# A four-layer Flamingo block: dense experts turned into experts by routing, with the routing inside the second attention and an unrolled feed-forward

## The reference, cut to what matters

```python
x = x + tanh(g_xattn[0]) * attention0(ln(x), ctx, ctx)       # 16 heads of 8
x = x + tanh(g_ffn[0])   * feed_forward0(ln(x))              # quantised rows, 128 -> 512, depthwise conv, silu, 512 -> 128
x = x + tanh(g_xattn[1]) * attention1(ctx, ln(x))            # latents attend to context and latents, 16 heads of 64, layer norm
x = x + tanh(g_ffn[1])   * experts(ln(x))

def experts(x):                                              # E = 8 experts, K = 2 chosen per row, 256 hidden
    gate = x @ Wg.T
    top_v, top_i = top_k(gate, 2)
    probs = softmax(top_v)
    for e in range(8):
        w_e = sum(probs * (top_i == e))                      # zero for the six that were not chosen
        h1, h2 = x @ W1[e].T, x @ W2[e].T
        out += (h1 * sigmoid(h1) * h2) @ W3[e].T * w_e
```

## Time and profile before

| | us |
|---|---|
| median of three runs | 1413.82 |
| lowest, highest | 1412.66, 1414.06 |
| the profiled execution, its own time | 1411.43 |
| its span, first to last instruction | 1409.6 |
| PE busy (granted clock 0.894 of full on average) | 1197.1 |
| DVE busy | 1099.3 |
| ACT busy | 930.5 |
| POOL busy | 856.1 |

### The profile page before, as it was taken

One profiled execution on the slowest core, in us unless ns is written; L12 is line 12 of the kernel. 1 busy time (PEld: TensorE's weight loads), 2 busy tenths in 40 slices (PEclk: granted clock), 3 DMA queues, 4 the chain that ended last, 5 costly groups with the idle time before them and its releaser, 6 DMA issues. The chain is left out here.

```text
span 1409.6 us, 39591 instructions
## 1 busy us (share of the span) xinstructions
PE 1197.1 (85%) x14741; PEld 902.5 (64%) x14741; DVE 1099.3 (78%) x2878; ACT 930.5 (66%) x1858; POOL 856.1 (61%) x823
## 2 busy tenths in 40 slices
PE   1578999949984599999999999999994688888887
PEld 1445777735652488888887878787873355555555
DVE  5888888867988666777767686868674799998996
ACT  0668999836654488778787878787872455454554
POOL 0251999942207366676666666666663477777778
PEclk9879555559995799999999999999997799999999
DMA  9100000000000021111111112111111000000000
GB/s 229 54 1 1 13 16 17 16 9 1 1 1 0 1 32 32 32 29 32 28 32 32 31 26 32 32 32 28 32 29 23 0 1 9 8 7 7 7 8 16
DMA packets 104027, 33.09 MB, mean 23 GB/s; under 512 B 88468, under 2 KB 102204, under 8 KB 103868
## 3 DMA queue, kind: packets, MB, share of 16 engines
q1 hardware_dynamic: 92827, 27.50, 9.6%
q10 hardware_dynamic: 11040, 3.42, 1.0%
HBM read 9.92 MB, written 2.10 MB: 9 GB/s over the span
## 5 line engine op out<-in xcount | busy, mean ns | idle before, releaser
L1173 POOL TENSOR_TENSOR attention_pl_l<-attention_probs_l,attention_ph_l 128x512 f16<-128x512 f32 x128 | 148.0, 1157 | 180.6 <-ACT attention_ph_l L1343 180.6
L1407 DVE TENSOR_REDUCE attention_negmax<-bank 128x2 f16<-128x410 f32 x256 | 137.7, 579 | 136.5 <-PE bank L1252 136.3
L1589 POOL TENSOR_TENSOR mixture_hidden_l<-mixture_hidden,mixture_hidden_h 128x512 f16<-128x512 f32 x128 | 148.3, 1159 | 74.9 <-ACT mixture_hidden_h L1676 74.9
L612 POOL TENSOR_TENSOR attention_probs_l<-attention_probs,attention_probs_h 77x512 f16<-77x512 f32 x128 | 145.3, 1152 | 52.7 <-ACT attention_probs_h L694 48.5
L1173 POOL TENSOR_TENSOR attention_pl_c<-attention_probs_c,attention_ph_c 77x512 f16<-77x512 f32 x128 | 147.4, 1152 | 0.0
L1685 ACT ACTIVATE mixture_tanh<-bank 128x512 f32<-128x512 f32 x128 | 76.4, 597 | 105.4 <-PE bank L1636 105.4
L1634 PE MATMUL bank<-mixture_xs,moeh 128*128 128x512 f16 x256 | 98.2, 383 | 31.9 <-DVE mixture_hidden L1767 31.9
L1267 PEld LDWEIGHTS bank<-identh,attention_negmax 128*128 128x128 f16 (+1 forms) x1024 | 83.3, 107 | 55.7
L1235 PE MATMUL bank<-layer_kv,ah 128*128 128x128 f16 x1024 | 108.8, 220 | 11.1 <-PEq L89 11.0
L1343 ACT ACTIVATE attention_probs_l<-bank 128x512 f32<-128x512 f32 x128 | 76.4, 597 | 56.9 <-PE bank L1267 56.9
L1263 PE MATMUL bank<-attention_th,layer_kv 128*128 128x512 f16 (+1 forms) x256 | 97.0, 379 | 14.6 <-issue 14.4
(11 more groups left out here) (325 smaller groups left out, 4787.8 us busy)
## 6 DMA issues: line engine op xcount, KB each, us to landing
X<-in_x SPq DMA_DIRECT2D x4, 512.0 KB, 9.2
out<-X SPq DMA_DIRECT2D x8, 256.0 KB, 2.3
attention_turned_h<-attention_heads_h SPq DMA_TRANSPOSE x96, 2.3
attention_turned_l<-attention_heads_l SPq DMA_TRANSPOSE x96, 2.4
ctx<-in_ctx SPq DMA_DIRECT2D x1, 1232.0 KB
setup_nat_w<-in_w SPq DMA_DIRECT2D x1, 1024.0 KB, 14.7
setup_nat_f<-in_fw ACTq DMA_DIRECT2D x2, 256.0 KB, 6.9
setup_nat_q<-in_q ACTq DMA_DIRECT2D x1, 512.0 KB, 7.9
```

Of the source, the lines that this page charges most:

```text
L612: pool.tensor_tensor(probs_l[:, n % SLOTS], probs[:, n % 2], probs_h[:, n % SLOTS], ALU.subtract).then_inc(p_split, 1)
L1173: last = pool.tensor_tensor(low[:, g % 2], whole[:, g % 2], high[:, g % 2], ALU.subtract)
L1407: last = dve.tensor_reduce(negmax[:, g, 2 * i:2 * i + 2], score[i], AX.X, ALU.max, negate=True)
L1589: pool.tensor_tensor(hidden_l[:, e % 4, j], hidden[:, e % 2, j], hidden_h[:, e % 4, j], ALU.subtract).then_inc(hid_lo, 1)
```

## The change

The mixture over all experts and the split ahead of it are removed. Instead each row is sent to its two experts and each expert computes only its own rows:

- In the setup a blank row pattern is made, and SP writes it over the whole of a table in DRAM, `tokens` (34,560 rows of 272 fp16 values). Further small constants are made by POOL.
- In the second attention the lists go nine sequences beyond the last one. For each batch of four sequences, DVE finishes the statistics of x and normalises, ACT and POOL write the high and low halves with the row's number (`pay`), SP transposes them by DMA, PE makes gates (`choose`), DVE finds the top two (`top_two`, `select`), PE counts the rows ahead of each (`number`), DVE makes places (`find`, `places`, `count_up`), and POOL sends 128 rows at a time to their places in `tokens` by indirect DMA (`send`, eight per batch). At the end DVE makes a table of 39 tiles: where each starts and whose expert it is.
- `experts` goes through 39 tiles of 256 rows. SP reads a tile transposed from `tokens`, ACT its row numbers; the weights are addressed by a register loaded from the table. POOL sends the outputs by indirect DMA to `outputs` in DRAM, in the order of the rows. After the last tile SP reads `outputs` back and DVE adds the two rows with their shares to x; ACT issues the stores.
- The feed-forward is written out without a loop. `to_channels` and `integers` are replaced by a POOL conversion (`unbias`) and a DMA transpose by SP; `project` comes two sequences behind and `residual` three.
- Ahead of the second attention the semaphores of the setup are cleared, and a barrier follows. The attention's outputs and `heads_out` use the room of the context, which is widened to 128 partitions.

The diff at its core:

```diff
+T = 256
+ROW = 2 * 128 + 16
+TILES = (2 * B * S + E * (T - 1)) // T
+ROWS = E * B * S + (TILES - 2 * B * S // T) * T
...
 # setup, sync
             sp.wait_ge(moe_in, 48)
+            sp.wait_ge(blank_in, 1)
+            sp.dma_start(w.tokens.rearrange("(t p) r -> p t r", p=128),
+                         w.blank[:].unsqueeze(1).broadcast_to([128, ROWS // 128, ROW])).then_inc(w.cleared, 16)
...
 # feed_forward0
+            def unbias(k, c):                                   # gpsimd
+                pool.wait_ge(biased_in, k * CH + (c + 1))
+                if late(k):
+                    pool.wait_ge(turned_in[c], 16 * k)
+                pool.tensor_scalar(whole[:, c], biased[:, c % 2], ROUND, None, ALU.subtract).then_inc(whole_in, 1)
...
+                    sp.dma_start_transpose(ints[:, c], whole[:, c]).then_inc(turned_in[c], 16)
...
-                    to_channels(k, c)
-                    if not (isinstance(k, int) and k == 0 and c == 0):
-                        project(k * CH + (c - 1), (c + CH - 1) % CH)
+                    there, *sequence = behind(k, c, 2)
+                    if there:
+                        project(*sequence)
...
 # attention1, gpsimd
+            def fill(k):
+                u = k % 2
+                pool.wait_ge(pay_hi, k + 1)
+                pool.iota(...).then_inc(numbered, 1)
+                pool.tensor_tensor(pay[:, u, :, :, D:2 * D], normed_x[:].unsqueeze(1).broadcast_to([S, 2, BATCH, D]),
+                                   pay[:, u, :, :, 0:D], ALU.subtract).then_inc(pay_lo, 1)
...
+                pool.indirect_dma_start(w.tokens, bass.IndirectOffsetOnAxis(ap=slot[:, u, i, c:c + 1], axis=0),
+                                        pay[:, u, i, c], None).then_inc(sent[u], 16)
...
 # attention1, vector: what a sequence's four units hold beside the old steps
+                    k = ending(b, 7)
+                    if k is not None and g == 2:
+                        aggregate_x(k)
+                        guess_x(k)
+                    if k is not None and g == 3:
+                        newton_x(k)
+                        newton_x(k)
+                    k = ending(b, 8)
+                    if k is not None and g == 0:
+                        newton_x(k)
+                        normalise_x(k)
+                    k = ending(b, 9)
+                    if k is not None and g == 1:
+                        top_two(k)
+                    if k is not None and g == 2:
+                        select(k)
+                    k = ending(b, 10)
+                    if k is not None and g == 0:
+                        find(k)
+                    if k is not None and g == 2:
+                        places(k)
+                        count_up(k)
+                    if k is not None and g == 3:
+                        shares(k)
...
 # experts
+            for n in range(TILES):                              # sync
+                row = sp.value_load(w.table[0:1, 0, n:n + 1], min_val=0, max_val=ROWS - T)
+                if n >= RX:
+                    sp.wait_ge(h_done, n - RX + 1)
+                sp.dma_start_transpose(xt[:, n % RX], w.tokens[bass.ds(row, T), 0:2 * D]).then_inc(x_in[n % RX], 16)
...
+            for n in range(TILES + LAG):                        # tensor
+                if n < TILES:
+                    rise(n, pe.value_load(w.table[0:1, 1, n:n + 1], min_val=0, max_val=MH * (E - 1)))
+                if n >= LAG:
+                    fall(n - LAG, pe.value_load(w.table[0:1, 1, n - LAG:n - LAG + 1], min_val=0, max_val=MH * (E - 1)))
...
+            for n in range(TILES + LAG + 1):                    # scalar
+                if n < TILES:
+                    squash(n)
+                if 1 <= n < TILES + 1:
+                    hidden_high(n - 1)
+                if n < TILES:
+                    number(n)
+                if n >= LAG + 1:
+                    copy_out(n - LAG - 1)
...
+            def send(n):                                        # gpsimd
+                pool.wait_ge(y_copied, n + 1)
+                pool.wait_ge(id_in[n % RI], 16 * (n // RI + 1))
+                for r in range(T // S):
+                    pool.indirect_dma_start(w.outputs, bass.IndirectOffsetOnAxis(ap=ids[:, n % RI, r].bitcast(UINT32), axis=0),
+                                            y_rows[:, n % RY, r], None, bounds_check=2 * B * S - 1,
+                                            oob_is_err=False).then_inc(y_out[n % RY], 16)
...
 # flamingo
+                nc.clear_and_free_semaphores(w.spent)
+                nc.all_engine_barrier()
                 attention1(nc, w, bank, kv)
-        with Memory(nc, "moe") as m:
-            xh, xl = m.sb("xh", [D, B, S], FP16), m.sb("xl", [D, B, S], FP16)
-            split_transposed(nc, w, bank, "split2", [...], before=row_scale(w))
-            mixture(nc, a, w, bank, xh, xl)
+        experts(nc, a, w, bank)
```

More of the change, by code:

```diff
@@ L1213, in _ @@
+                    for q in range(2 * BATCH):
+                        k = ending(b - (3 + q) // G, 10)
+                        if k is not None and g == (3 + q) % G:
+                            send(k, q)
+            pool.memset(pay[:, :, :, :, 2 * D + 2:ROW].rearrange("p u i c r -> p (u i c) r"), 0.0).then_inc(padded, 1)
             sequences(body)
-            heads_low(B - 1, 1)
-            gain(B // BATCH - 1)
-            residual(B // BATCH - 1)
+            for u in range(2):
+                pool.wait_ge(sent[u], 16 * 2 * BATCH * (BATCHES // 2))
@@ L1231, in _ @@
+            sequences(body)
         @block.tensor
@@ new lines, in count_up, with shares @@
+            def count_up(k):
+                u = k % 2
+                link(dve.tensor_reduce(tally[:], sel[:, u].rearrange("p c e -> p e c"), AX.X, ALU.add))
+                if k == 0:
+                    link(dve.tensor_copy(so_far[:], tally[:]))
+                else:
+                    link(dve.tensor_tensor(so_far[:], so_far[:], tally[:], ALU.add))
+            def shares(k):
+                first, second = (w.share[:, batch(k), i] for i in range(2))
+                dve.wait_ge(gexped, k + 1)
+                link(dve.tensor_scalar(first, expd[:], 1.0, None, ALU.add))
+                link(dve.reciprocal(first, first))
+                dve.tensor_scalar(second, first, -1.0, 1.0, ALU.mult, ALU.add)
@@ L1810, in flamingo @@
+            for n in range(TILES):
+                send(n)
 def flamingo(nc, a):
```

829 lines of the change are left out of this document (448 added, 381 removed).

## The result

The changed kernel takes 1418.26 us (median of 6 runs, 1417.50 to 1421.92), the kernel before 1413.94 in the same session: ratio 1.0036, 95% interval 1.0025 to 1.0047. It is a little slower; 1342 us was forecast. The profiled execution took 1417.5 us, span 1415.4, against 1411.4 and 1409.6.

What follows compares the result with a forecast made beforehand. PE and DVE were taken to share the bound in the mixture, PE alone in the second attention. 1411.4 + 48 - 14 + 2 + 30 - 21.7 + 38 - 302.7 + 149 = 1340.0, plus 2.4: 1342 us, range 1268 to 1430.

Steps and rivals of the forecast that it cites:

- The routing inside the second attention, +30: Second attention: added routing costs 30 us, as 5 PE work, 17 heavy DVE units, 8 POOL; bounds 5 and 60.
- Clearing, +48: Setup: SP's DMA that blanks the token table holds SP and delays the barrier by 48 us; bounds 11 to 70.
- the longer end: Setup clearing: SP is held until 88% of the runs are through, free at 113, 56 us late.
- Rival (b): Setup: SP hands the clearing over without being held, +11, total 1305 us; chance 0.11.
- Feed-forward, -14: Feed-forward: removed fp32 transposes and DVE conversions save 0.44 us a sequence, 14 us; bounds 0 to -20.
- Clearing of semaphores, +2: Ahead of the second attention: clearing semaphores and a barrier cost 2 us; bounds 0 to 6.
- Last batch's chain, +38 for the 21.7 removed: Between attention and experts: the last batch's routing, 38 us, replaces the 21.7 us split, net +16.3; bounds +30 to +55.
- Experts, 149 us: Experts to the end: 39 tiles at 2.8 us, 109, plus 40 around them, replacing 302.7 us.
- Rival (a): POOL's indirect sends are slow and decide, kernel slower; 1575 us at 3.1 a send; chance 0.12 together with (e).
- (c): Experts: PE falls to its 1.2 GHz level, 4.0 us a tile, +47, total 1389 us; chance 0.10.
- (d): Attention hides the routing but PE's work (+5), and expert tiles go at DVE's 2.1 us; total 1290; chance 0.11.
- (e): Experts: the tiles' chain doesn't overlap, 8.1 us a tile, total 1549 us; chance 0.12 together with Rival (a).

Runs made afterwards that it cites:

- e1_retimed: The changed kernel with only the places of the routing's steps between the attention's units moved apart; 1378.9 us, ratio 0.9750 to the kernel before.
- h1_placed: e1_retimed with the experts' second layer three tiles behind, feed-forward conversions on ACT, and some small DVE operations moved to where POOL is idle; 1335.9 us, ratio 0.9451.
- e3_no_sends: The changed kernel without the attention's 64 indirect sends, so the experts compute on blank rows; 1439.1 us, ratio 1.0172, attention 706.2 us.
- f3_ff_act: e1_retimed with the feed-forward's 32 conversions ahead of the DMA transposes on ACT instead of POOL; 1377.0 us, ratio 0.9735.
- h2_tail_paced: h1_placed with DVE's and POOL's order behind the attention changed and the experts' sends waiting for a later tile's tanh; 1333.0 us, ratio 0.9430.
- g1_no_out_sends: e1_retimed without the 78 indirect sends of the experts' rows, the read-back taken from the input; 1335.6 us, ratio 0.9444.
- e2_moved: The changed kernel with the row normalisation moved from DVE to ACT and the places' products to POOL, schedule unchanged; 1423.8 us, ratio 1.0071.

## Why the prediction was wrong

The sign came out wrong by one term. **"The routing inside the second attention, +30"** was 122.9. That step priced DVE's additions as four heavy units a batch, 17 in all, and PE's as work alone, 5. It had no term for waits that the change itself puts into PE's queue and none for the clock, and operations of DVE that POOL holds were named but didn't enter the price. The runs split the 122.9:

- 71.9 went with the steps' places (e1_retimed): the waits that the change adds to PE's queue, what they made late behind them, and one pair of DVE operations that stood beside a busy POOL. With the waits the clock came back, 22.5 of the 71.9. The step named none of them. `project` waits for `gates_read` and `rank_read`, `number` for `selected`, and each of these is made by DVE in the same unit or the one before. Everything of the unit that stands behind them on PE, and with it the next maxima, moves by the wait. This could be read from the diff: for each new wait, how many units lie between the writer's place and the waiter's.
- 24.1 are DVE operations held by POOL (h1_placed against e1_retimed), about 9 of them as PE's busy time with the clock back at 1.00. The row of 2.19 us for a 0.16 us operation was read, and stands in the step's 9 to 14 us of DVE's work; but the price went by 0.93 a unit, whatever POOL did beside it. It should have priced the routing's steps, by what POOL has in a row at their place: a held one took up to 3.52 us.
- 26.9 remain in h1_placed, near the 30 that were forecast: PE is busy 4.8 us more, for which 5 was the price, and stands 22.1 more, for which it was 17 + 8.

That nearness is partly luck. The 8 were for POOL, a filling and a send that run over; the sends cost the attention nothing (e3_no_sends), the filling wasn't taken out, and the 17 were too few.

**Clearing, +48:** +1.0. The held issuer of 5.50 us was taken as the rule for a large DMA. An issue of 18.8 MB in 34,560 runs took 0.41 us, so the count of runs ahead of an issuer is not what the 5.50 showed, and the longer end, which the step took for the right one, was wrong. Rival (b) was right and its price of 11 still too high. This miss of 47 lies on the other side: without it the sum would have been 1295, and 123 short.

**Feed-forward, -14:** -4.6, the first attention included. PE's busy time fell by 11.5 (107.0 to 95.48), and it stands more: before the projection 7.2 us for the residual and 4.1 for the transposed integers. The step took both bounding engines' savings as the stage's. f3_ff_act shortens the stage by 3.1, so the conversion that it named as the risk is not the main part; the rest wasn't tried.

**Clearing of semaphores, +2:** +1.3.

**Last batch's chain, +38 for the 21.7 removed:** +26.1 instead of +16.3. (The chain's own terms add up to 36.7.) It was counted from the attention's end as if nothing stood before it. The seventh batch's gating stood ahead of the last projection on PE, 12.7 us, and landing and barrier took 8.0 for 2.5. The eight sends took 9.9 for 10. Yet e1_retimed, where the gating stands behind the last projection, gained only 3.8 in this stretch, and mending DVE's and POOL's order 1.5 more (h2_tail_paced): other waits end at nearly the same time, and which bounds the rest is open.

**Experts, 149 us:** 161.9. The tile was forecast at 2.8 and took 2.9; a send takes 0.98 and the next starts 1.27 to 1.29 after it, for the 1.25: 112.7 for 109. What lay around the tiles was 49.2 for 40. Rival (a) (slow sends) fell by the size of the sends, (c) by the granted clock of 0.96 in the tiles, (d) and (e) by the attention and by the pace of the tiles.

1418 lies in the range of 1268 to 1430, but by luck and not for the reason that the range gave: its upper part stood for a low clock in the experts and for slow sends, while the loss came from waits in order. The chances don't quite add up either: 0.12 for (a) and (e), 0.01 of it level, leaves 0.11 for slower and 0.88 for faster.

## What to carry to other kernels

When steps of a second chain are threaded between the units of a full pipeline, list every wait that they add to the bounding engine, and lay the writer at least one whole unit before the waiter; here that was worth 72 us of 123, with one held pair of operations and the clock that came back included. Small VectorE operations that read SBUF have no price of their own beside a busy GpSimd: look at what GpSimd has in a row at that place, and put them in its gap. Where the bounding engine begins to stand, look at its granted clock too: in this attention it made about 32 us of the 123. And when a stage is mended, measure the stages behind it again: of the 72.9 us that e1_retimed won up to its first tile, 28.1 were given back by tiles that had been even before.

## What the runs showed of the hardware that was not expected

- Beside indirect sends of GpSimd a TensorE result can be seen late by others. With four sends in a row ACT started 2.66 us after the last matmul's end; without sends (g1_no_out_sends) it followed at once, in 38 of 38 waits. The same code of the experts ran at an even pace of 3.1 us a tile in the changed kernel and in pairs of 8.3 in e1_retimed, e2_moved and e3_no_sends. The four runs of e1_retimed lie within 1.8 us, so the pace doesn't seem to be drawn anew in each run; what starts the pairs is open.
- A VectorE operation can be held for more than one GpSimd instruction: 3.52 us, over three in a row, for a product that takes 0.18 alone.
- The sends took 961 to 1239 ns, over 64 of them, beside a busy DVE. The Trainium skill, "SBUF — State Buffer", section "A bandwidth-pool intuition that's wrong (but worth ruling out)", has a GpSimd DMA go from 620 to 3100 ns beside a DVE copy; no send here showed that, though DVE had only short operations beside them.
- A DMA of 18.8 MB in runs of 544 B landed 71.1 us after its issue, 264 GB/s, and let its issuer go after 0.41.
